# Transposed probabilities in a PSUM bank of their own; exps and gelus ahead of the cell state's tanh

## What is computed

```python
x = x + attn(lstm(x, cond), Wq, Wkv_down, Wk_up, Wv_up, Wout)   # 16 heads, latent of 32, causal, softmax
x = x + ffn(gru(x, cond), gate_w, w1, b1, w2, b2)               # 8 experts, top 2, exact gelu

# lstm, one step            i, f, o = sigmoid(...), g = tanh(a[:, 3H:])
next_c = f * prev_c + i * g
next_h = o * jnp.tanh(next_c)
# gru, one step; every fourth step h goes through tanh(h @ Wp + bp) besides
h_new = (1.0 - z) * h + z * jnp.tanh(concat([x_t, r * h]) @ Wh + bh)
# ffn: all 8 experts are computed for each token, the best two are kept
h = gelu(einsum('td,ndh->tnh', xt, w1) + b1);  out_all = einsum('tnh,nhd->tnd', h, w2) + b2
```

## Time and profile before

| | |
|---|---|
| three runs | 852.35, 856.5, 860.57 us (median 856.5) |
| profiled execution | 853.5 us, its span 851.6 us |
| PE busy | 679.1 us, 80% of the span |
| PE weight loads | 603.3 us, 71% |
| DVE busy | 398.2 us, 47% |
| ACT busy | 354.2 us, 42% |
| POOL busy | 131.5 us, 15% |
| chain that ended last | PE 63%, DVE 16%, ACT 13%, issue 6% |
| mean granted TensorE clock | 0.836 |

### The profile page before, as it was taken

How to read it: one execution, slowest core, us unless ns; L and a number is a source line. 1 busy time by engine, 2 the same in 40 slices (tenths; PEclk the granted TensorE clock), 3 DMA queues, 4 the chain that set the end, 5 groups by cost and what they waited for, 6 DMA issues and landing times.

```text
span 851.6 us, 19294 instructions
## 1 busy us (share of the span) xinstructions
PE 679.1 (80%) x7090; PEld 603.3 (71%) x7090; DVE 398.2 (47%) x2308; ACT 354.2 (42%) x1240; POOL 131.5 (15%) x339
## 2 busy tenths in 40 slices
PE   6968978877788777887788778887888787788888
PEld 3536756777678667776777677776877677777787
DVE  2454553443644455445554455545555444434332
ACT  1434323343533454335533564334533563343333
POOL 3033022100420022101220032101220032000000
PEclk8886966665667998789977998789977998599999
DMA  9100000000000000000000000000000000000000
GB/s 292 76 1 2 2 1 1 2 1 1 2 1 2 4 2 2 2 7 2 2 1 1 8 2 2 1 8 2 1 2 1 8 1 1 1 8 1 1 8 10
DMA packets 5531, 10.07 MB, mean 12 GB/s; under 512 B 1827, under 2 KB 4527, under 8 KB 5054
## 3 DMA queue, kind: packets, MB, share of 16 engines
q1 hardware_dynamic: 4686, 6.47, 2.1%
q10 hardware_dynamic: 752, 2.37, 1.1%
HBM read 7.79 MB, written 1.05 MB: 10 GB/s over the span
## 4 chain that ended last, share of the span: by engine, by line
PE 63%; DVE 16%; ACT 13%; issue 6%; DMA 1%; SPq 0%; POOL 0%; DVEq 0%; POOLq 0%; ACTq 0%
PE pY L443 16%; PE pH L443 13%; PE pG L443 9%; PE pV L538 7%; PE pV L443 6%; ACT hid L798 5%; PE pL L443 5%; PE pC L443 5%; PE pS L443 4%; DVE gB L1010 2%; DVE On L919 2%; ACT L798 2%; ACT gC L810 2%; DVE ghi L1013 2%; DVE glo L1016 2%
## 5 line engine op out<-in xcount | busy, mean ns | idle before, releaser
L443 PE MATMUL pY<-w,hid 128*128 128x128 f32 x1024 | 161.2, 311 | 0.0
L443 PEld LDWEIGHTS pY<-w,hid 128*128 128x128 f32 x1024 | 146.5, 220 | 2.3
L417 POOL COPY qbd<-qh 32x256 f16<-32x256 f16 x256 | 101.5, 396 | 196.0 <-PE pS L443 180.0
L1001 DVE SCALAR_TENSOR_TENSOR gRZ<-gT,g 128x32 f32<-128x32 f32 x128 | 25.9, 203 | 199.9 <-ACT gT L805 199.4
L798 ACT ACTIVATE hid<-pH,b 128x256 f32<-128x256 f32 (+1 forms) x288 | 111.9, 445 | 12.0 <-PE pH L443 11.8
L538 PE MATMUL pV<-ident,P 128*128 128x128 f32 x256 | 59.8, 378 | 68.1 <-DVE On L919 66.4
L443 PE MATMUL pH<-ghi,w1hi 128*128 128x256 f16 (+1 forms) x288 | 77.1, 273 | 43.5 <-ACT hid L798 42.7
L805 ACT ACTIVATE gT<-pG 128x32 f32<-128x32 f32 x128 | 25.2, 197 | 187.0 <-PE pG L443 186.9
L538 PEld LDWEIGHTS pV<-ident,P 128*128 128x128 f32 x256 | 39.1, 190 | 71.9 <-ACT P L781 59.4
L443 PE MATMUL pH<-ghi,w1lo 128*128 128x256 f16 (+1 forms) x288 | 78.0, 276 | 0.0
L443 PE MATMUL pH<-glo,w1hi 128*128 128x256 f16 (+1 forms) x288 | 77.9, 276 | 0.0
(11 more groups left out here) (156 smaller groups left out, 1558.9 us busy)
## 6 DMA issues: line engine op xcount, KB each, us to landing
w<-in_w SPq DMA_DIRECT2D x2, 2048.0 KB, 10.7
out<-acc SPq DMA_DIRECT2D x16, 64.0 KB, 1.5
xT<-in_xT ACTq DMA_DIRECT2D x1, 960.0 KB, 9.6
hid<-in_WqT ACTq DMA_DIRECT2D x1, 512.0 KB, 5.4
hid<-in_Wout ACTq DMA_DIRECT2D x1, 512.0 KB, 7.6
lWh<-in_lWh SPq DMA_DIRECT2D x1, 256.0 KB, 2.7
lWx<-in_lWx SPq DMA_DIRECT2D x1, 256.0 KB, 9.2
gWh<-in_gWh SPq DMA_DIRECT2D x1, 192.0 KB, 7.1
```

The lines of the kernel that those rows point to most:

```text
L417: pool.tensor_copy(qbd[r, n % 2, :, :, q, :], qh[r, p % 2, :, 2 * u:2 * u + 2, :, :].rearrange("p l b (g c) t -> p l (b g) (c t)", g=2)).t ...
L443: return nc.tensor.matmul(o, lhsT=lhsT, rhs=rhs, start=start, stop=stop, skip_group_check=True)
L1001: V.scalar_tensor_tensor(gRZ[:, :, :], gT[:, :, :], 1.0, g8[:, at:last + 1:last - at, :], ALU.add, ALU.mult).then_inc(g_rh, 1)
```

## The change

The four transposes of a unit's probabilities write pH[1], the bank of the experts' second half, and no longer pV. They now wait until ACT has copied the turned probabilities of the unit before, and for the gelus of all experts issued so far; the wait for On moves to the values. The second half of an expert's first product waits for the copy of the unit turned last. `keep_warm` writes pH[0]. On ACT, all four exps of a unit stand together ahead of the tanh of the cell state, and so do the gelus of the second half.

```diff
--- before.py
+++ after.py
@@ -447,7 +447,7 @@
 
             def keep_warm(k, n):
                 for _ in range(n):
-                    mm((pY if k < 5 else pH[1])[:, :], still[:, 0:128], still[:, :], start=True)
+                    mm((pY if k < 5 else pH[0])[:, :], still[:, 0:128], still[:, :], start=True)
 
             def bank_c(nq, npj, nr):
                 if nq:
@@ -530,18 +530,23 @@
                     last = mm(S, flat(qbd[:, n % 2, 1, j, :, :]), lathi[:, b, 0:L])
                 last.then_inc(s_mm, 1)
 
-            def turn_probs(n):
+            def turn_probs(n, k):
                 pe.wait_ge(exp_done, 4 * (n + 1))
                 if n:
-                    pe.wait_ge(on_done, n)
+                    pe.wait_ge(pt_done, n)
+                ups = len([at for at in UP_AT if at < k])
+                if ups:
+                    pe.wait_ge(gelu, 4 * ups)
                 for j in range(4):
-                    last = nc.tensor.transpose(pV[:, 128 * j:128 * (j + 1)], P[:, n % 3, j, :], ident[:, :])
+                    last = nc.tensor.transpose(pH[1][:, 128 * j:128 * (j + 1)], P[:, n % 3, j, :], ident[:, :])
                 last.then_inc(pt_mm, 1)
 
             def values(n):
                 p, u = divmod(n, NU)
                 pe.wait_ge(pt_done, n + 1)
                 pe.wait_ge(latn_done, p + 1)
+                if n:
+                    pe.wait_ge(on_done, n)
                 for j in range(4):
                     last = mm(V_[:, j, 0:LD + 1], PTs[:, n % 2, j, :], latN[:, 2 * u + j // 2, :], start=(j == 0))
                 last.then_inc(o_mm, 1)
@@ -597,8 +602,11 @@
                 mm(pC[:, 0:E], flat(g8[:, GS * n:GS * (n + 1), :]), gateW[:, :], start=True)
                 nc.tensor.transpose(pC[:, 128:256], x1T[:, n * TOK:(n + 1) * TOK], ident[:, :]).then_inc(r_mm, 1)
 
-            def expert_up(m, e, cp):
+            def expert_up(m, e, cp, k):
                 n = 2 * (E * m + e) + cp
+                turned = len([j for j in range(k + 1) if unit_at(j, O_T) is not None])
+                if cp == 1 and turned:
+                    pe.wait_ge(pt_done, turned)
                 if n == 0:
                     pe.wait_ge(set_w1, E)
                 tiles = tiles_of(m)
@@ -662,9 +670,9 @@
                     l_step(t)
 
                 if unit_at(k, O_T) is not None:
-                    turn_probs(unit_at(k, O_T))
+                    turn_probs(unit_at(k, O_T), k)
                 for m, e in UP_AT.get(k, []):
-                    expert_up(m, e, 0)
+                    expert_up(m, e, 0, k)
                 if (g + 1) % GS == 0 and 0 <= g + 1 < T:
                     g_fill((g + 1) // GS)
                 if prop and (k, "B") not in DOWN_AT and unit_at(k, O_T) is not None:
@@ -681,7 +689,7 @@
                 if k in ROUTES:
                     route_x(ROUTES[k], k)
                 for m, e in UP_AT.get(k, []):
-                    expert_up(m, e, 1)
+                    expert_up(m, e, 1, k)
                 if k == 1:
                     pe.wait_ge(loaded_fold, 4 * 16)
                     for h in range(H):
@@ -770,21 +778,21 @@
                 A(qh[:, par, 0, :, :, t0:t0 + GS], pC[:, :].rearrange("p (g s b) -> p b g s", g=HG, b=B),
                   ACT.Copy, scale=1.0 / SP).then_inc(q_hi, 1)
 
-            def exps(n, pair):
+            def exps(n):
                 L = keys(n // NU)
                 act.wait_ge(mx_done, n + 1)
                 if n == 0:
                     act.wait_ge(cleared, NCLEAR)
                 if n >= 3:
                     act.wait_ge(pt_mm, n - 2)
-                for j in (2 * pair, 2 * pair + 1):
+                for j in range(4):
                     A(P[:, n % 3, j, 0:L], S_of(L)[:, j, :], ACT.Exp, bias=mx[:, j:j + 1]).then_inc(exp_done, 1)
 
             def pt_copy(n):
                 act.wait_ge(pt_mm, n + 1)
                 if n >= 2:
                     act.wait_ge(o_mm, n - 1)
-                A(PTs[:, n % 2, :, :].rearrange("p j q -> p (j q)"), pV[:, :], ACT.Copy).then_inc(pt_done, 1)
+                A(PTs[:, n % 2, :, :].rearrange("p j q -> p (j q)"), pH[1][:, :], ACT.Copy).then_inc(pt_done, 1)
 
             def activate(m, e, cp):
                 n = 2 * (E * m + e) + cp
@@ -812,14 +820,12 @@
                     act.wait_ge(l_gates, t + 1)
                     A(lT[:, 0:4, :], pL[:, :, t % GS, :], ACT.Tanh, scale=1.0 / SP).then_inc(l_tanh, 1)
                 if unit_at(k - 1, O_S) is not None:
-                    exps(unit_at(k - 1, O_S), 0)
+                    exps(unit_at(k - 1, O_S))
+                for m, e in UP_AT.get(k - 1, []):
+                    activate(m, e, 1)
                 if t < T:
                     act.wait_ge(l_c, t + 1)
                     A(lC[:, :], lT[:, 4, :], ACT.Tanh, scale=0.5).then_inc(l_tc, 1)
-                if unit_at(k - 1, O_S) is not None:
-                    exps(unit_at(k - 1, O_S), 1)
-                for m, e in UP_AT.get(k - 1, []):
-                    activate(m, e, 1)
                 setup(k)
                 if 0 <= g < T - 1 and g % 4 == 3:
                     act.wait_ge(g_prop, g // 4 + 1)
```

## The result

The changed kernel took 715.7 us (median of four runs, 713.3 to 723.5) against 858.5 (four runs). The ratio is 0.836, 95% interval 0.827 to 0.844.

What follows compares the result with a forecast made beforehand. TensorE, 80% busy, was held mainly by waits for room in PSUM: transposes for On, experts' first product for a gelu. 853.5 - 62 (gap) - 25 (gelus) + 5 (place 2) - 25 (clock) gave 746 us, range 726 to 785.

Steps and rivals of the forecast that it cites:

- The gap (62 us): Places 4 to 10: TensorE's 66.4 us wait for On before the transposes goes, 4 us come back; 62 us gained.
- the chain from values to values: Places 4 to 10: next values wait for the copy behind the cell's tanh, 4.15 us; doesn't bite unless the clock rises.
- The clock (25 us): Places 4 to 10: without the idle gap TensorE's clock mostly stays high; 38 us at most, two thirds taken, 25 us.
- Rival B: Seven stretches, places 4 to 10: the clock keeps alternating; 771 us, up to 785; chance 0.27.
- Gelus (25 us): Expert steps: gelus ahead of the cell's tanh cut the first product's wait by 0.94 of 1.40 us; 25 us gained.
- Place 2 (5 us): Table load and gelus ahead of the cell's tanh delay the next step's gRZ 1.0 us in five blocks; 5 us lost.
- The early steps (nothing taken): Seven LSTM-only steps: grouped exps delay the cell's tanh by up to 0.5 us, small gaps go; nothing taken.
- C: Another wait, such as ScalarE's exps, holds the transposes; 833 us, milder forms 785 to 833; chance 0.13.
- D: Expert steps: new table switches if tanh and gelu share no table, 105 us added; 901 us; chance 0.03.

## Why the prediction was wrong in size

**The gap (62 us).** Right as a mechanism: the wait went, nothing of that size took its place, the chain from values to values measured 3.9 where 4.15 was put. The run with the wait kept shows that this one wait carries all of it. By PE's idle time in the stretches it came to 54 us; 4 us were put for what comes back, and 11.4 us of idle time were left.

**The clock (25 us): the step that failed.** The forecast took 38 us as the most that the clock could give, and two thirds of that. PE's busy time in the stretches fell by 57 us. The most was mis-sized: of 21 us that a stretch ran at half clock it called 12 us heavy (six groups of down products, 0.91 us each, 5.5 in all) and "the rest as small products whose time hardly changes". The run with the filled gap measured 9.2 us in that stretch at a full clock, 44% of the low time and not 26%. The down products gave 2.8 of it, half of the 5.5, as there are five such groups and not all of them ran low. The transposes gave 2.6, which the forecast held for nothing: its rows had four of them at 1.09 us at the low level and none at the high one, where they take 0.63. Projections, fills of the input, scores and the first expert product gave most of the rest. Over all stretches the filling gave 49 us, with the seventh not held; the 57 us of the changed kernel are a little more. The second part of the error was to take two thirds: the clock rose to 0.95 to 1.00 in six of the seven stretches and 0.89 in the first.

**Why the rise.** Rival B fell: PE without the gap kept the clock. Filling with idle work shows that it was PE's idle time at that place and not what the steps compute that let it fall. The forecast's reason for it was weaker than it looked: gaps between heavier products did not "never" cost the clock. Its row showed 16 us of expert steps at 1.00; the first block of them, steps 43 to 49, ran at 0.54 in the kernel before and at 0.74 in the changed one:

```profile
179.76:219.87 40.11, 32.62 (x314) 30.35 (x314) 17.18 (x109) 15.17 (x62) 4.63 (x13) 0.54 0.01 2
157.94:189.15 31.21, 26.56 (x314) 24.50 (x313) 16.48 (x107) 14.96 (x62) 4.72 (x13) 0.74 0.01 2
```

**Gelus (25 us).** The wait came out right, 25 us less for pH, and so did the time, 26.5 in the changed kernel and 26.1 alone; but the time is in part luck. The first block, above, gave 8.9 us, most of it with its clock. The other six gave 17.6: place 0 became 0.94 us shorter, as forecast, while place 1 became 0.3 longer and the clock now fell at place 11 in more blocks.

**Place 2 (5 us).** Right place and right chain, but the size was twice that: 10.1 us. The 1.0 us of waiting came true; the step's work at half clock after the longer idle time came on top. The same effect that was counted as a gain in the stretches was not looked for as a loss here. The table load again took 1.28 us, with the gelus 0.02 us behind it.

**The early steps (nothing taken).** They took 9.2 us less. Steps 0 to 33 took 102.1 to 107.0 us in the five profiled executions that have the program of before there (104.4 on average), and 97.6 to 100.6 in the six that turn the probabilities into pH[1] (98.3). So some 6 us are the change's and the rest is the difference between executions. It isn't the wait for On: the run with the wait kept took 97.9. Which part of the change it is stays open.

**The sum.** The 29 us beyond the forecast are 32 more for the clock, 8 less for the gap, 1.5 more for the gelus, 5 lost at place 2, and 8.5 gained ahead of step 34, where nothing was put.

**The rivals.** C fell with the timeline after, where the transposes start at 445.90 and the exps at 446.20, and with the run of the exps alone. D, table switches, had no ground: 26 loads in the trace of the changed kernel as before, 1283 ns each. The range ended too early on the fast side because its lower end was the clock term's mis-sized bound.

## What to carry over

A wait that only guards a bank costs its own length and, in this kernel, the slower clock of TensorE's work around it; here the two were about equal, 54 and 57 us, and the same effect has to be looked for where an edit makes an idle time longer, even by a microsecond. To size it, count all of TensorE's work that ran at the low level and not only the longest groups (here 9.2 of 21 us came back), or fill the idle time with products into an idle bank and measure. An edit that does next to nothing alone, like the exps here, can be worth some 20 us once another wait is gone. And a row that shows one window at the full clock doesn't say that such steps always keep it: ask for the others too.

## What the runs showed of the hardware

Extra products with zeros in an idle time of 1.2 to 1.9 us a step made a kernel 7% faster (800 against 862 us), with the data's own work unchanged. The granted clock of one stretch of those steps went from 0.78 to 1.00, in the seven from 0.70 to 0.79 up to 0.91 to 1.00, but for one at 0.75. Transposes filling the same time lifted it too, to between 0.74 and 0.89 in six of the seven (the seventh stayed at 0.72). In most blocks the changed kernel's clock still fell at three places: at place 3 behind 2.45 us of idle time and at place 11 at the end of one of 1.11, both because of a table load on ScalarE (1283 ns each), and at place 9 behind one of 0.6 to 0.8 us that three operations of VectorE cause.
